# An attention pipeline reordered slot by slot: weighted sum in four places, triangle cleared under two signals, causal mask added from half the array's height

## The chip, the cores and the metric

The kernel is written in Bass and runs on one core of a Trainium2 chip. The metric is the device time of one launch, in microseconds (us). The names of the engines are those of the profile: PE is TensorE (PEld its weight loads), DVE is VectorE, ACT is ScalarE, POOL is GpSimd, and SP is SyncE, which only issues DMA transfers here.

## The reference, cut to what matters

Two transformer-like layers run one after the other; the change touches only the first one's differential attention (8 batches, 512 tokens, 16 heads, two attention maps a head):

```
q1, q2, k1, k2 = heads of x @ Wq1, x @ Wq2, x @ Wk1, x @ Wk2     # 8 features each
v = heads of x @ Wv                                             # 16 features each
a1 = softmax(where(causal, q1 k1^T * scale, -inf))
a2 = softmax(where(causal, q2 k2^T * scale, -inf))
out = (a1 - lam * a2) @ v
merged = layernorm(out) * (1 - LAM_INIT)
return merged @ Wo
```

After it come a feed-forward layer, a state-space scan and a mixture of experts. The change leaves their code as it is.

## The kernel before, in words

The attention works in **rounds**, one for each batch (r = 0 to 7), with a preparing round r = -1 ahead and a draining round r = B behind. A round has 8 **slots** (g = 0 to 7), and each slot works on a **group** of two heads, that is four attention maps. The work is software-pipelined by an order written out by hand. In slot g:

- the *first scores* of group g (`first_pair`, L755): five pairs of 128x512 units, computed only to find each query's largest score. DVE takes the maximum of each unit (L1036), and after ten units the negated maxima (`qneg`, L1047);
- POOL splits the maxima of group g-1 into two bf16 parts (`nsp`, L630 and L632), PE turns them (`turn_neg`, L860), ACT copies them (`nparts`, L704), and SP sends them as two more rows of the query stack (L595);
- the *second scores* of group g-2 (`second_pair`, L807), transposed and with the maximum already subtracted, in five pairs, and ACT's exponential of each unit (L679) into `pT`. POOL clears what lies above the diagonal (L639, three instructions, all counted on the semaphore `masked`);
- the *weighted sum* of group g-3 (`product`, L822): four chunks of keys, c = 0 to 3, with 512, 384, 256 and 128 query columns, summed in the one bank `ob`. It needs `pT` cleared, POOL's copy `vs` of the values (L656), and `ob` read by ACT;
- ACT's copy of the sum of group g-4 out of `ob` (`o_sb`, L685), PE's turn of it (`turn_o`, L852), and ACT's copy of the turned sum (L695).

Beside these a round carries the **preparation** of the next batch: `turn_x` (slot 0), four `project` products of 128x512 (L878, slots 1 to 4), each cut into three bf16 parts by ACT (the high part, L709), DVE (the rest `res`, L1041), ACT (the middle part, L689) and POOL (the lowest part, L660) and stored by SP (L604, six DMAs each), and four `value` products (L884, slots 3 to 6). It also carries the **post-processing** of the batch before: reciprocals (L998), POOL's products and sum (L644 to L648), squares, their sum, a Newton iteration for the inverse root and `merged` (L1010 to L1020) on DVE, then in slot 7 `turn_m0`, `turn_m1` (L892) and the eight products of `wo` (L899), whose result DVE gates and adds to x (L1050, L1054).

The first scores use three PSUM banks (`p1b`), the second scores three others (`p2b`), in turn: a pair of units t may be written when unit 2t-2 has been read. The side products share one bank, `auxb`: each waits until the one before it has been read (`aux_free`). Every engine takes its instructions strictly in the order in which `slot` of its block issues them, so that order sets what waits behind what.

The causal mask of the diagonal units is added by PE ahead of the scores (`mask`, L759): the identity is the stationary operand and `causal`, a 128x512 tile with -3e38 above the diagonal, is the moving one. There are four of these in a slot, for two of the five pairs:

```
def mask(bank):
    pe.matmul(bank[:, :], k.identb[:, :], causal[:, :, :].rearrange("p c t -> p (c t)"), start=True, ...)
```

The order of PE in a slot is given by `AUX`, `AV_AT` and the loop over t: second pair ahead of first pair, the first pair of the *next* slot at the end of this one.

Of the kernel before, what the change touches and what calls it, by code (L numbers as in the profile page):

```python
# [21 lines left out]
P = 128  # L22
# [204 lines left out]
class AttentionTiles:  # L227
# [3 lines left out]
    def __init__(self, nc, ctx, k):  # L231
# [10 lines left out]
        self.causal = sb("causal", [P, TILES, P], BF16)  # L242
# [25 lines left out]
def setup(nc, d, k, t):  # L268

    with ExitStack() as ctx:  # L270
# [50 lines left out]
        def _(pool):  # L321
# [11 lines left out]
            pool.memset(t.causal[:, :, :], 0.0).then_inc(t.slots_set, 1)  # L333
            pool.memset(t.ks[:, :, :, :], 1.0).then_inc(t.slots_set, 1)
            pool.wait_ge(t.slots_set, 3)
            pool.affine_select(out=t.causal[:, :, :], in_=t.causal[:, :, :], compare_op=ALU.is_ge, fill=NEG, base=0,
                               pattern=[[0, TILES], [-1, P]], channel_multiplier=1).then_inc(t.slots_set, 1)
# [107 lines left out]
AUX = {"turn_o": 1, "turn_neg": 2, "project": 3, "value": 4, "turn_x": 4, "turn_m0": 3, "turn_m1": 4, "wo": 5}  # L445
CHUNKS = ((0, 0, S), (1, P, S), (2, 2 * P, S), (3, 3 * P, S))
# [15 lines left out]
def bank_of(g, u):  # L462
    return (g * UNITS + u) % BANKS
# [39 lines left out]
def attention(nc, d, k, t):  # L503
# [3 lines left out]
    with ExitStack() as ctx:  # L507
# [6 lines left out]
        def sem(name):  # L514
            return ctx.enter_context(nc.semaphore(name))

        wqk, causal, xn, hT, parts, res, vst, qs, ks, vs, pT, bmax = (t.wqk, t.causal, t.xn, t.hT, t.parts, t.res, t.vst, t.qs, t.ks, t.vs, t.pT, t.bmax)
# [12 lines left out]
        first_unit, first_read, second_unit, exp_done, masked, vs_ready, av_done, o_read = (  # L530
            sem(n) for n in ("first_unit", "first_read", "second_unit", "exp_done", "masked", "vs_ready", "av_done", "o_read"))
# [43 lines left out]
        def _(sp):  # L575
# [13 lines left out]
            def slot(r, g, on, prep, post):  # L589
# [7 lines left out]
                if prep and 2 <= g < 6:  # L597
                    b, j = r + 1, g - 2
# [14 lines left out]
        def _(pool):  # L613
            for s, n in CREDITS.items():
                pool.sem_inc(s, n)
            def slot(r, g, on, prep, post):
# [4 lines left out]
                alone = isinstance(r, int) and r == B  # L621
                if on(1):
# [6 lines left out]
                    pool.sem_inc(passed, 1)  # L629
                    pool.tensor_copy(high, lowest).then_inc(nsp_high, 1)  # L630
                    pool.wait_ge(nsp_high, G + 1)
                    pool.tensor_tensor(mid, lowest, high, ALU.subtract).then_inc(nsp_ready, 1)  # L632
                if on(3):
                    r3, g3 = lagged(r, g, 3)
                    a = g3 % 2
                    pool.wait_ge(exp_done, (r3 * GROUPS + g3 + 1) * UNITS + BANK_CREDITS)
                    pool.sem_inc(passed, 1)
                    for block_ap, n in ((pT[:, a, :, 0:P], UNITS), (pT[:, a, 1:8:2, 384:512], 4), (pT[:, a, 8:10, 256:384], 2)):
                        pool.affine_select(out=block_ap, in_=block_ap, compare_op=ALU.is_ge, fill=0.0, base=0,  # L639
                                           pattern=[[0, n], [1, P]], channel_multiplier=-1).then_inc(masked, 1)  # L640
# [5 lines left out]
                if post and g == 5 and not alone:  # L646
                    pool.wait_ge(pool_own, pb * 2 + 2)
                    pool.tensor_tensor(og[:, :, :], og[:, :, :], o2[:, :, :], ALU.add).then_inc(og_ready, 1)  # L648
                if on(2):
                    r2, g2 = lagged(r, g, 2)  # L650
                    G = r2 * GROUPS + g2
                    a = g2 % 2
                    pool.wait_ge(aux_read, aux_use(r2 - 1, 6, "value") + 1)
                    pool.wait_ge(av_done, G + 1)
                    pool.sem_inc(passed, 1)
                    pool.tensor_copy(vs[:, a, :, :, :], vst[:, r2 % 2, :, 2 * g2:2 * g2 + 2, :]).then_inc(vs_ready, 1)  # L656
                if prep and 2 <= g < 6:
                    j, J = g - 2, (r + 1) * 4 + g - 2
# [1782 lines left out]
```

## Time and profile before

| what | us |
|---|---|
| median of 3 runs | 1569.78 |
| lowest, highest run | 1566.35, 1570.98 |
| the profiled execution, its own time | 1568.49 |
| its span in the trace | 1566.7 |
| PE busy over the span | 1265.0 (81%) |
| DVE busy | 1162.6 (74%) |
| ACT busy | 1080.8 (69%) |
| POOL busy | 799.6 (51%) |
| first score of the attention starts at | 59.9 |
| first scores end at | about 747 |

The span counts from the first to the last instruction of the core. "Busy" is the union of an engine's instructions; matmuls that run side by side in different parts of the array are counted once there. The mean granted clock of PE is 0.92 of full speed. A timeline row gives start, duration, engine, line, operation, output and inputs, the count of merged instructions, and in brackets how long the engine had been idle before it and who released it.

### The profile page before, as it was taken

The numbers are of one execution on the slowest core, as the hardware profiler recorded it, in microseconds if no ns is written. First come the engines' busy times: TensorE is split into PE (matmuls) and PEld (weight loads), VectorE is DVE, ScalarE is ACT, GpSimd is POOL, SyncE is SP. The second block draws the span as 40 slices with busy tenths as digits, with TensorE's granted clock in tenths as the row PEclk, the third lists the DMA queues.
The fourth block names the chain that finished last, engine by engine and source line by source line (L and its number), as shares of the span: only waits on it lengthen the run. The fifth ranks groups of instructions, "written<-read, shape, count | busy, mean of one in ns | idle before, by whom it ended". The sixth has DMA issues, their size and how long they took to land. (4 is left out here: it accounts for less than half of the span.)

```text
span 1566.7 us, 25959 instructions
## 1 busy us (share of the span) xinstructions
PE 1265.0 (81%) x8518; PEld 567.3 (36%) x8581; DVE 1162.6 (74%) x2000; ACT 1080.8 (69%) x1712; POOL 799.6 (51%) x721
## 2 busy tenths in 40 slices
PE   4588878788888888787777857778668999999998
PEld 3133333333333333333335522323223444444443
DVE  5667676767677676778859689999995677766663
ACT  2167767767675767676667788888537877787776
POOL 3033433525252442534200158988955777787777
PEclk8579999999998999999879979889988999999999
DMA  5332322213132222311000178978748777777785
GB/s 135 92 92 63 89 66 69 86 50 105 42 94 61 75 80 64 91 43 32 2 0 1 56 227 281 311 276 272 266 154 191 177 191 178 177 188 183 192 192 128
DMA packets 123688, 198.60 MB, mean 127 GB/s; under 512 B 24604, under 2 KB 60088, under 8 KB 123576
## 3 DMA queue, kind: packets, MB, share of 16 engines
q1 hardware_dynamic: 122136, 195.08, 43.7%
q10 hardware_dynamic: 1440, 2.10, 0.4%
q8 instruction: 62, 1.02, 0.3%
q14 instruction: 50, 0.41, 0.1%
HBM read 167.76 MB, written 28.84 MB: 125 GB/s over the span
## 5 line engine op out<-in xcount | busy, mean ns | idle before, releaser
L1036 DVE TENSOR_REDUCE bmax<-p1b 128x4 f32<-128x512 f32 x640 | 410.6, 686 | 125.9 <-PE p1b L755 123.2
L679 ACT ACTIVATE pT<-p2b 128x512 f32<-128x512 f32 x640 | 349.2, 603 | 184.2 <-PE p2b L807 183.0
L2179 POOL TENSOR_TENSOR hid_l<-e_hid,w_experts 128x1024 f16<-128x1024 f32 (+1 forms) x136 | 281.3, 2084 | 105.1 <-ACT w_experts L2314 104.2
L2413 DVE TENSOR_TENSOR e_hid<-ub,w_experts 128x1024 f32<-128x1024 f32 x128 | 155.8, 1223 | 122.5 <-ACT ub L2325 113.1
L630 POOL CAST nsp<-qneg 128x16 bf16<-128x16 f32 x64 | 12.7, 198 | 425.0 <-DVE qneg L1047 425.0
L822 PE MATMUL ob<-pT,vs 128*32 128x512 f32 (+3 forms) x2048 | 192.1, 462 | 1.9 <-POOL pT L639 1.2
L1882 PE MATMUL yb<-ch,ident 128*128 128x512 f32 x256 | 138.4, 674 | 49.7 <-POOL ch L1852 49.3
L807 PE MATMUL p2b<-w_high 50*128 50x512 bf16 (+3 forms) x1024 | 130.4, 314 | 48.0 <-ACT pT L679 48.0
L2314 ACT ACTIVATE w_experts<-e_hid 128x1024 f16<-128x1024 f32 (+1 forms) x136 | 139.4, 1026 | 39.1 <-DVE e_hid L2413 39.0
L2325 ACT ACTIVATE ub<-ub 128x1024 f32<-128x1024 f32 (+1 forms) x136 | 133.9, 985 | 37.6 <-PE ub L2230 35.8
L639 POOL TENSOR_SCALAR_AFFINE_SELECT pT<-pT 128x1280 f32<-128x1280 f32 (+2 forms) x192 | 145.3, 790 | 11.7 <-ACT pT L679 11.6
L755 PE MATMUL p1b<-w_high 48*128 48x128 bf16 (+2 forms) x1792 | 133.1, 253 | 19.9 <-DVE bmax L1036 19.8
L2228 PE MATMUL ub<-w,w_high 128*128 (+1 forms) x264 | 100.9, 382 | 22.9 <-DVE e_hid L2413 13.7
L1962 ACT ACTIVATE dA<-dt,nA 128x511 f32<-128x511 f32 x128 | 85.4, 712 | 45.5 <-DVE hs L2025 33.6
L759 PE MATMUL p1b<-causal,identb 128*128 128x512 bf16 x193 | 81.1, 422 | 37.2 <-DVE bmax L1036 25.1
L807 PEld LDWEIGHTS p2b<-w_high 50*128 50x128 bf16 x1024 | 34.7, 95 | 196.7 <-ACT pT L679 149.9
L1852 POOL TENSOR_TENSOR ch<-hs,crow 128x1024 f32<-128x1024 f32 x40 | 93.9, 2352 | 17.2 <-DVE hs L2025 16.8
L2229 PE MATMUL ub<-w,w_high 128*128 (+1 forms) x264 | 100.8, 382 | 0.0
L2230 PE MATMUL ub<-w,w_low 128*128 (+1 forms) x264 | 100.6, 381 | 0.0
L2228 PE MATMUL e_yb<-w_experts,w_high 128*128 128x512 f16 x264 | 100.1, 379 | 0.5 <-POOL hid_l L2179 0.5
L2230 PE MATMUL e_yb<-w_experts,w_low 128*128 128x512 f16 x264 | 100.1, 379 | 0.0
L2229 PE MATMUL e_yb<-hid_l,w_high 128*128 128x512 f16 x264 | 100.1, 379 | 0.0
(308 smaller groups left out, 2265.0 us busy)
## 6 DMA issues: line engine op xcount, KB each, us to landing
w_experts<-shares SPq DMA_DIRECT2D x256, 256.0 KB, 4.3
brow<-bc_rows SPq DMA_DIRECT2D x64, 512.0 KB, 4.0
crow<-bc_rows SPq DMA_DIRECT2D x64, 512.0 KB, 5.2
q_stacks<-w_low SPq DMA_DIRECT2D x96, 128.0 KB
k_stacks<-w_low SPq DMA_DIRECT2D x96, 128.0 KB
w_high<-q_stacks SPq DMA_DIRECT2D x128, 96.0 KB, 2.3
w_high<-k_stacks SPq DMA_DIRECT2D x128, 96.0 KB, 2.3
w_high<-nparts SPq DMA_DIRECT2D x128, 4.0 KB
```

Of the source, the lines that this page charges most:

```text
L639: pool.affine_select(out=block_ap, in_=block_ap, compare_op=ALU.is_ge, fill=0.0, base=0, pattern=[[0, n], [1, P]], channel_multiplier=-1). ...
L679: act.activation(pT[:, g2 % 2, stored(w), :], p2b[bank_of(g2, w)][:, :], ACT.Exp, scale=SCALE).then_inc(exp_done, 1)
L807: mm = pe.matmul(p2b[bank_of(g, 2 * t + j)][:, at:at + S - c * P], ks[rows, slot, head, c * P:(c + 1) * P], qs[rows, slot, head, c * P:S], ...
L822: mm = pe.matmul(ob[32 * m:32 * m + 32, q0:q1], vs[:, a, c, m // 2, :], pT[:, a, u, at:at + q1 - q0], start=(n == 0), stop=(n == len(CHUNK ...
L1036: dve.tensor_reduce(to, bank, AX, ALU.max).then_inc(first_read, 1)
L1882: mm = pe.matmul(yb[:, :], k.ident[:, :], ch[:, m % 4, j, :], start=False, stop=(m == PAIRS - 1 and j == 1), skip_group_check=True)
L2179: pool.tensor_tensor(flat(hid_l[:, rounded(p), 0:n, :]), flat(hid[:, place(p), 0:n, :]), rounded_half(p, 0, n), ALU.subtract).then_inc(spl ...
L2228: pe.matmul(to, w[0], high, start=start, stop=False, skip_group_check=True)
L2229: pe.matmul(to, w[0], low, start=False, stop=False, skip_group_check=True)
L2230: return pe.matmul(to, w[1], high, start=False, stop=stop, skip_group_check=True)
L2314: act.activation(rounded_half(p, 0, n), flat(hid[:, place(p), 0:n, :]), ACT.Copy).then_inc(hid_rounded, 1)
L2413: dve.tensor_tensor(h, u, flat(share[:, p % SHARES, :, :]), ALU.mult).then_inc(hid_ready, 1)
```

## The change

1. **PE's order.** The first pair of a slot is issued in the slot itself, and each pair t is first scores, then second scores. The weighted sum's chunks go to four places: chunk 1 after pair 1, chunks 3 and 2 after pair 2, chunk 0 (512 columns) last. `project` and `turn_m0` move behind pair 0, `turn_x` and `turn_m1` behind pair 1, `turn_o` from behind pair 1 to behind pair 3, `wo` behind pair 4 and ahead of chunk 0.
2. **ACT's order** goes by single units: `o_sb` and the high part right after the first exponential, the middle part and `nparts` after the fifth, the copy of the turned sum after the seventh, the values after the tenth. The middle part is made in the project's own slot, not one later.
3. **POOL's order.** `vs` first, then the sum of `og` (slot 5), then `nsp`, then the clearing of the last two units of group g-3 under a signal of its own (`masked_last`), the products of slot 4, the lowest part, and at the end the clearing of units 0 to 7 of group g-2, one slot earlier than before. Only chunk 2 waits for `masked_last`.
4. **DVE's order.** The rest `res` behind unit 3 instead of 6, the normalisation of x behind unit 0 of slot 0, and the steps of the post-processing at other units.
5. **SP** stores the parts one slot earlier.
6. **The mask.** `later`, a 128x384 tile, is now the stationary operand (64 rows of it) and the identity, 64 rows broadcast to 256 columns, the moving one: four products of 64 rows by 256 columns for a pair, instead of two of 128 rows by 512.

```diff
-        self.causal = sb("causal", [P, TILES, P], BF16)
+        self.later = sb("later", [P, 3, P], BF16)
...
-            def mask(bank):
-                pe.matmul(bank[:, :], k.identb[:, :], causal[:, :, :].rearrange("p c t -> p (c t)"), start=True, stop=False, skip_group_check=True)
+            def mask(bank, j, half):
+                rows = slice(HALF * j, HALF * j + HALF)
+                keys = bank[:, :].rearrange("p (c t) -> p c t", c=TILES)[:, :, HALF * half:HALF * half + HALF]
+                pe.matmul(keys, later[rows, 1 + half - j, :], k.identb[rows, rows].unsqueeze(1).broadcast_to([HALF, TILES, HALF]),
+                          start=(half == 0), stop=False, skip_group_check=True)
...
                 bank_free(r, g, 2 * t + 1)
                 if kind == DIAGONAL:
-                    mask(bank[1])
+                    for half in range(2):
+                        for j in range(2):
+                            mask(bank[j], j, half)
...
-AV_AT = (2, 3, 4, 4)
-O_COPY_AT, OT_AT, NEG_COPY_AT, HIGH_AT, MID_AT, HT_AT, V_COPY_AT, MT_AT = 0, 1, 2, 3, 1, 4, 4, (3, 4)
-RES_AT = 6
-POST_AT = ((4, 0), (5, 6), (5, 8), (6, 0), (6, 2), (6, 4), (6, 6), (6, 8))
+CHUNK_FIRST, CHUNK_LAST = 1, 0
+O_COPY_AT, HIGH_AT, MT_AT, HT_AT, MID_AT, NEG_COPY_AT, OT_AT, V_COPY_AT = 0, 0, (1, 3), 2, 4, 4, 6, 9
+RES_AT, NORM_AT = 3, 0
+POST_AT = ((3, 9), (5, 4), (5, 8), (6, 4), (6, 5), (6, 6), (6, 7), (6, 9))
...
+                if c == CHUNK_FIRST:
+                    pe.wait_ge(masked, 2 * G + 2)
                     pe.wait_ge(vs_ready, G + GROUPS + 2)
                     pe.wait_ge(o_read, G + 1)
+                if c == 2:
+                    pe.wait_ge(masked_last, G + 1)
```

In the rows below, `p1b` is a bank of first scores, `p2b` one of second scores, `ob` the weighted sum and `auxb` the side products.

**PE, the start of slot 6 of a full round.** Before (the slot's first pair was already issued behind the chunks of slot 5, and is shown as the first two rows):

```order
L759 MATMUL p1b<-causal,identb 128x512 x2
L755 MATMUL p1b<-w_high 128x128 x8
L807 MATMUL p2b<-w_high 128x512 x2
L807 MATMUL p2b<-w_high 128x384 x2
L807 MATMUL p2b<-w_high 128x128 x2
L755 MATMUL p1b<-w_high 128x384 x2
L755 MATMUL p1b<-w_high 128x128 x2
L852 MATMUL auxb<-ident,o_sb 128x128 x4
L759 MATMUL p1b<-causal,identb 128x512
L807 MATMUL p2b<-w_high 128x512 x2
L759 MATMUL p1b<-causal,identb 128x512
L755 MATMUL p1b<-w_high 128x128 x8
```

And now:

```order
L767 MATMUL p1b<-identb,later 128x4x64 x4
L760 MATMUL p1b<-w_high 128x128 x8
L813 MATMUL p2b<-w_high 128x512 x2
L760 MATMUL p1b<-w_high 128x384 x2
L760 MATMUL p1b<-w_high 128x128 x2
L813 MATMUL p2b<-w_high 128x384 x2
L813 MATMUL p2b<-w_high 128x128 x2
L831 MATMUL ob<-pT,vs 32x384 x4
L767 MATMUL p1b<-identb,later 128x4x64 x4
L760 MATMUL p1b<-w_high 128x128 x8
L813 MATMUL p2b<-w_high 128x512 x2
```

The turn of `o_sb` between pairs 1 and 2 gave way to chunk 1 of the weighted sum, the masks of a pair stand together, and first and second scores have changed places.

**POOL, from the products of slot 4 to the clearing of slot 5.** Before:

```order
L660 TENSOR_TENSOR w_low<-w_low 128x512 [waits mid_ready]
L630 CAST nsp<-qneg 128x8x2 [waits qneg_ready,aux_done]
L632 TENSOR_TENSOR nsp<-qneg,nsp 128x8x2 [waits nsp_high]
L639 AFFINE_SELECT pT<-pT 128x10x128 [waits exp_done]
L639 AFFINE_SELECT pT<-pT 128x4x128
L639 AFFINE_SELECT pT<-pT 128x2x128
L648 TENSOR_TENSOR og<-og,o 128x1024 [waits pool_own]
L656 COPY vs<-w_experts 128x256 [waits aux_read,av_done]
```

And now:

```order
L660 TENSOR_TENSOR w_low<-w_low 128x512 [waits mid_ready]
L645 AFFINE_SELECT pT<-pT 128x8x128 [waits exp_done]
L645 AFFINE_SELECT pT<-pT 128x4x128
L628 COPY vs<-w_experts 128x256 [waits av_done,aux_read]
L631 TENSOR_TENSOR og<-og,o 128x1024 [waits pool_own]
L639 CAST nsp<-qneg 128x8x2 [waits aux_done,qneg_ready]
L641 TENSOR_TENSOR nsp<-qneg,nsp 128x8x2 [waits nsp_high]
L645 AFFINE_SELECT pT<-pT 128x4x128 [waits exp_done]
```

`vs` and the sum into `og` now stand ahead of the split of the maxima, and eight of the ten units are cleared before the slot ends.

## Rows read from the trace of the kernel before

**Rows 1.** Windows, a slot without preparation: length, busy PE, PEld, DVE, ACT, POOL, then PEclk

```profile
699.61:708.19 8.58, 7.22 (x93) 3.10 (x90) 6.70 (x12) 6.65 (x13) 2.99 (x6) 1.00 0.17 46
```

**Rows 2.** Windows, one full round: slots 1 to 6, 7, then 0; the round; the last round

```profile
329.90:340.62 10.72, 8.92 (x100) 3.71 (x100) 7.29 (x12) 7.39 (x15) 2.99 (x6) 1.00 0.17 47
340.62:350.69 10.07, 8.35 (x95) 3.45 (x90) 7.20 (x12) 7.58 (x15) 4.15 (x7) 1.00 0.18 55
350.69:360.77 10.08, 8.61 (x87) 3.39 (x82) 7.20 (x13) 7.89 (x16) 4.15 (x7) 1.00 0.38 118
360.77:371.96 11.19, 9.05 (x92) 3.63 (x92) 7.90 (x13) 7.97 (x16) 7.99 (x9) 1.00 0.32 96
371.96:382.75 10.79, 8.54 (x100) 3.65 (x100) 9.02 (x14) 7.37 (x15) 7.40 (x8) 1.00 0.37 115
382.75:394.04 11.29, 9.63 (x95) 3.81 (x90) 10.73 (x25) 7.20 (x14) 2.99 (x6) 0.85 0.39 120
394.04:403.05 9.01, 7.76 (x90) 3.62 (x86) 6.61 (x11) 7.63 (x15) 2.99 (x6) 1.00 0.07 17
403.05:418.46 15.41, 12.82 (x107) 6.25 (x109) 9.01 (x17) 7.41 (x14) 2.99 (x6) 0.78 0.10 28
318.21:406.61 88.40, 73.52 (x740) 31.42 (x748) 64.96 (x116) 60.75 (x120) 35.64 (x55) 0.94 0.25 74
...
674.46:750.67 76.21, 62.59 (x711) 27.44 (x718) 61.81 (x107) 54.56 (x107) 29.43 (x50) 0.98 0.12 33
```

**Rows 3.** Timeline, the slot of rows 1: PE and ACT up to the turn of o_sb

```profile
699.67 0.38 PE L807 MATMUL p2b<-w_high 50*128 50x512 bf16 x2
...
700.15 1.09 ACT L679 ACTIVATE pT<-p2b 128x512 f32<-128x512 f32 x2 [1.07 <-PE p2b L807]
...
701.12 0.69 ACT L685 ACTIVATE o_sb<-ob,factor 128x512 f32<-128x512 f32 x1
...
701.86 0.42 PEld L852 LDWEIGHTS auxb<-ident,o_sb 128*128 128x128 f32 x4 [0.73 <-ACT o_sb L685]
```

**Rows 4.** Timeline, the same slot: the rest of PE's queue, and four reductions in a row

```profile
702.99 0.39 PE L759 MATMUL p1b<-causal,identb 128*128 128x512 bf16 x1
...
703.31 0.40 PE L755 MATMUL p1b<-w_high 48*128 48x128 bf16 x8
...
703.86 1.02 PE L822 MATMUL ob<-pT,vs 128*32 128x512 f32 x5
...
704.82 0.39 PE L807 MATMUL p2b<-w_high 50*128 50x384 bf16 x4
...
705.04 0.38 PE L755 MATMUL p1b<-w_high 48*128 48x384 bf16 x4
...
705.46 2.62 DVE L1036 TENSOR_REDUCE bmax<-p1b 128x4 f32<-128x512 f32 x4 [0.43 <-PE p1b L755]
706.14 0.11 PEld L807 LDWEIGHTS p2b<-w_high 50*128 50x128 bf16 x4 [0.62 <-ACT pT L679]
```

**Rows 5.** Timeline, a slot with preparation: the project product and the rest

```profile
336.24 1.13 PE L878 MATMUL auxb<-w_low,wqk 128*128 128x512 f32 x2
...
338.03 0.69 DVE L1041 TENSOR_TENSOR w_low<-auxb,w_low 128x512 f32<-128x512 f32 x1 [1.00 <-ACT w_low L709]
```

**Rows 6.** Timeline, the start of a slot 0, after the products of wo

```profile
408.99 0.61 PE L755 MATMUL p1b<-w_high 48*128 48x384 bf16 x4 [1.68 <-DVE bmax L1036]
```

**Rows 7.** Timeline, the slot of rows 1: the rows of the maxima on their way

```profile
704.06 0.59 ACT L704 ACTIVATE nparts<-auxb 8x512 bf16<-8x512 bf16 x1
704.67 1.27 SPq L595 DMA_DIRECT2D w_high<-nparts  x2
```

**Rows 8.** Windows: where their bytes move; then a slot of round 0, and one two slots later

```profile
706.50:707.00 0.50, 0.50 (x14) 0.23 (x12) 0.47 (x2) 0.43 (x1) 0.00 (x0) 1.00 0.03 8
...
91.00:102.40 11.40, 10.41 (x79) 3.59 (x78) 6.92 (x11) 7.35 (x14) 4.11 (x7) 0.70 0.37 112
113.00:122.00 9.00, 7.65 (x89) 3.38 (x90) 6.74 (x12) 7.27 (x15) 4.15 (x7) 1.00 0.34 103
```

More of the change, by code:

```diff
@@ L621, in slot @@
                 alone = isinstance(r, int) and r == B
+                if on(2):
+                    r2, g2 = lagged(r, g, 2)
+                    G = r2 * GROUPS + g2
+                    a = g2 % 2
+                    pool.wait_ge(aux_read, aux_use(r2 - 1, 6, "value") + 1)
+                    pool.wait_ge(av_done, G + 1)
+                    pool.tensor_copy(vs[:, a, :, :, :], vst[:, r2 % 2, :, 2 * g2:2 * g2 + 2, :]).then_inc(vs_ready, 1)
+                if post and g == 5 and not alone:
+                    pool.wait_ge(pool_own, pb * 2 + 2)
+                    pool.tensor_tensor(og[:, :, :], og[:, :, :], o2[:, :, :], ALU.add).then_inc(og_ready, 1)
                 if on(1):
@@ L645, in slot @@
                     pool.tensor_tensor(o2[:, :, :], o[:, :, 1, :], rcv[:, :, 1].unsqueeze(2).broadcast_to(full), ALU.mult).then_inc(pool_own, 1)
[L646 to L648 removed]
+                if prep and 1 <= g < 5:
+                    j, J = g - 1, (r + 1) * 4 + g - 1
+                    pool.wait_ge(mid_ready, J + 1)
+                    pool.tensor_tensor(parts[:, j % 2, 2, :], res, parts[:, j % 2, 1, :], ALU.subtract).then_inc(split_ready, 1)
                 if on(2):
                     r2, g2 = lagged(r, g, 2)
[L651 removed]
                     a = g2 % 2
[L653 to L658, printed above, removed]
[L659 to L660 removed]
+                    pool.wait_ge(exp_done, (r2 * GROUPS + g2) * UNITS + 8 + BANK_CREDITS)
+                    clear_future(pT[:, a, 0:8, 0:P], [[0, 8]], masked)
+                    clear_future(pT[:, a, 1:8:2, 384:512], [[0, 4]], masked)
             rounds(pool, slot)
@@ L714, in slot @@
                         act.activation(mT[:, c, :], auxb[:, :], ACT.Copy).then_inc(aux_read, 1)
[L715 removed]
+                    if u == V_COPY_AT and prep and 3 <= g < 7:
                         c = g - 3
@@ new lines, in weigh @@
+                def weigh(c):
+                    if on(3):
+                        product(*lagged(r, g, 3), c)
+                pairs(0)
+                if 1 <= g < 5:
+                    side("project")
+                if g == GROUPS - 1:
+                    side("turn_m0")
+                pairs(1)
+                weigh(1)
+                if g == 0:
+                    side("turn_x")
+                if g == GROUPS - 1:
+                    side("turn_m1")
+                pairs(2)
@@ L943, in _ @@
+                side("turn_neg")
+                weigh(3)
+                weigh(2)
+                pairs(3)
+                side("turn_o")
+                pairs(4)
+                if 3 <= g < 7:
+                    side("value")
+                if g == GROUPS - 1:
+                    side("wo")
+                weigh(0)
             rounds(pe, slot)
@@ L951, in slot @@
                 G = r * GROUPS + g
-                if prep and g == 0 and (not isinstance(r, int) or r >= 0):
-                    dve.wait_ge(aux_done, aux_use(r - 1, 0, "turn_x") + 1)
-                    for c in range(TILES):
-                        ins = normalize(dve, k, xn[:, c, :], b * TILES + c)
-                    ins.then_inc(xn_ready, 1)
                 if isinstance(r, int) and r < 0:
@@ L1036, in slot @@
                         dve.tensor_reduce(to, bank, AX, ALU.max).then_inc(first_read, 1)
+                    if prep and (g, u) == (0, NORM_AT) and r >= 0:
+                        dve.wait_ge(aux_done, aux_use(r - 1, 0, "turn_x") + 1)
+                        for c in range(TILES):
+                            ins = normalize(dve, k, xn[:, c, :], b * TILES + c)
+                        ins.then_inc(xn_ready, 1)
                     if prep and u == RES_AT and 1 <= g < 5:
```

129 lines of the change are left out of this document (52 added, 77 removed).

## The prediction

> **What bounds the kernel now.** I read the windows by slot first, then the timeline of one slot, then the windows of the odd slots. The change lies in the attention, which is some 690 of the 1566.7 us; what follows it is left as it is.
>
> In a slot with nothing beside the pipeline [rows 1] TensorE is busy 7.22 of 8.58 us, VectorE 6.70 and ScalarE 6.65. No engine is full, TensorE is nearest. A full round takes 88.40 us, with TensorE busy 73.52, VectorE 64.96 and ScalarE 60.75 [rows 2]. So the bound is TensorE's queue and the waits in it. The timeline shows the one real gap of the plain slot: the second scores start at 699.67, the first exponential 0.48 later, ScalarE does two of them before it copies `o_sb` (0.97), and the turn of it starts 0.74 after that copy began [rows 3]. That is 2.19 us in which TensorE has one pair of each kind to do. From there its queue is dense [rows 4]. The other losses of a round are in slots 5 and 6, where VectorE is busy 9.02 and 10.73 us, and in slots 7 and 0 (9.01 + 15.41 us), where VectorE waits for `wo`, then normalises, while the granted clock is 0.78 [rows 2]; there TensorE stands 1.68 us for a bank [rows 6].
>
> **The change, part by part.**
>
> *Masks.* A full-height mask costs 0.32 us from its start to that of the scores behind it (702.99 to 703.31), four in a slot: about 1.2 us. The same 512 columns of half-height scores cost 0.22 (704.82 to 705.04) [rows 4]. That two half-height products with different rows run side by side is seen in the scores: eight of 128 columns take 0.40 us including the last one's latency. A pair's four products of 256 columns should therefore stream in 2 x 0.107 = 0.21 us, and I charge 0.3 with the first weight load. The bounds: 0.2 (nothing but streaming) and 0.6 (two full masks as now, no gain). I take 0.3, since it is next to the 0.22 row. Two pairs: 0.6 in place of 1.2, so TensorE's own work in a plain slot falls from 7.2 to 6.6 us.
>
> *Plain slot.* I walk TensorE's queue from the masks of pair 0. Masks 0.3, scores 0.24: second scores at 0.55. First exponential at 1.03 (+0.48), `o_sb` at 1.57, since now only one exponential (half of 1.09) stands ahead of it; the sum's chunk 1, which needs `ob` free, can start at 2.3 (+0.74) [rows 3]. Pair 1 fits in between: its first scores wait for the maximum of unit 0 (0.3 + 0.43 + 0.65 = 1.4, a reduction taking a quarter of 2.62 [rows 4]), its second ones for the exponential until 1.7. From 2.3: chunk 1 0.78, masks and pair 2 0.3 + 0.33 + 0.25, `turn_neg` 0.12, chunks 3 and 2 0.78, pair 3 0.47, `turn_o` 0.5, pair 4 0.57 with 0.1 of waiting for a maximum, chunk 0 1.06. The next slot begins at 7.6, and I take 7.7: 0.9 less than 8.58, of which 0.6 are masks and 0.3 the copy behind one exponential. The neighbours: VectorE needs ten reductions of 0.65 and 0.24 for `qneg`, 6.8; ScalarE about 6.9. Both fit in 7.7 but have under 1 us left, so no larger gain can come from TensorE.
>
> *Project, slots 1 to 4.* The product is 1.13 us long [rows 5]. Behind pair 0 it fills the wait for the first maximum (0.8 to 1.4), so 0.4 to 0.5 of it shows. The high part delays ScalarE by 0.6, and with it the exponentials of pair 1; the rest (0.69) sits behind unit 3 and holds `turn_neg` until 4.3. Walked through, the next slot starts at 8.4. With a value product (0.62 between pair 4 and chunk 0, slots 3 and 4): 9.1. Now these four slots take 42.1 us [rows 2]; then 35.0.
>
> *Slots 5 and 6* are VectorE's: 6.8 of its own, 2.5 of squares and sum in slot 5, 3.9 in slot 6. I expect 9.4 and 10.2 in place of 10.79 and 11.29 [rows 2], for its waits at the slot ends shrink but its work stays. The moved queues: GpSimd's sum into `og` (2.4 us) stands ahead of `nsp` in slot 5, and slot 4 ends late there (its products, lowest part and clearing come to 8 to 9 us). `nsp` is then ready some 3.5 us into the slot, `turn_neg` is due at 4: covered, but it costs what it is late. SyncE's six stores (3.7 us of issuing) come one slot earlier behind `split_ready`, and the next rows of maxima 4 us after: covered.
>
> *Slots 7 and 0.* `wo` runs behind pair 4, while VectorE still has two maxima and `qneg` to do, and chunk 0 runs while VectorE gates and adds; before, both stood in the way of the next slot. Walk: slot 7 11.3, slot 0 8.7, so 20.0 in place of 24.4 [rows 2]. The idle stretch of rows 6 should go.
>
> *The sum.* Round: 35.0 + 9.4 + 10.2 + 20.0 = 74.6. The same walk done on the slot of 10.07 gives 9.6, 4% too short, so I add 3%: 77. Six such rounds: 6 x (88.4 - 77) = 68. The last round, without preparation [rows 2]: 76.2 to 71, 5. Round 0: its first slots run at a clock of 0.5 to 0.7 and take 11.4 [rows 8], where masks cost twice; 1.5 each for five slots, 1 each for three: 10. The preparing round has the middle part ahead of the values: 1.5. The drain: 1. Together 85.5 us off 1568.5, the profiled execution's own time: 1483. The median of the runs shown lies 1.3 above that execution, which changes nothing.
>
> **A rule on the masks.** The full-height mask's 0.32 against 0.22 for the same columns at half height [rows 4] is a step of 0.1 where the height of the tile changes. The Trainium skill, TensorEngine Tiling (Array Packing), Key Properties, says that changing the tiling mode drains the engine. By that rule, the trace agrees.
>
> **The rivals.**
>
> *A. Masks cheaper still.* The drains between masks and scores vanish altogether, so a mask pair costs 0.2: 0.1 less, twice in 62 slots with TensorE as the bound, 12 us more: 1471. For it the 0.22 row; against it that pair 0 and pair 2 follow the sum, whose tiles are of another shape, so one change stays at each. 0.12.
>
> *B. Masks no cheaper.* The four half products run one behind the other, as their banks and weight loads alternate; 0.25 more for each pair, 0.5 a slot, 54 slots: 27 us, 1510. Against it: the scores of rows 4 alternate in the same way, side by side. This is also the case in which that part of the change does not do what it says. 0.08.
>
> *C. The rows of maxima come late.* `nparts` starts at 704.06, and the last of its bytes move in the window 706.5 to 707.0, 2.8 us later, with 4.2 to the second scores that need them [rows 7, 8]. In the new slot it is 3.6 (4.7 to 8.3), so 0.8 is left. If ScalarE comes to `nparts` later than walked, TensorE stands still at the start of the next slot. At 0.7 us in each slot that is 43 us: 1526. Its cousins, a late clearing or a late `vs`, would cost alike. 0.12.
>
> *D. The clock, slower than before.* TensorE fell to its lower level (1.2 GHz of 2.4) after idle stretches [rows 2, 6], and a slot at mean 0.70 took 11.4 against 9.0 at 1.00 [rows 8]. The change takes a third of the streamed mask work away and puts small waits (0.6 at pair 0, 0.4 at chunk 1) into each slot. At the lower level a slot's 6.6 us of work grows by some 5. Then it decides from 17 slots on (85/5); in half of the 64 slots it costs 160 and gives 1643, and if only the slots 5 to 0 of each round are hit, 28 of them, 140: about 1623. Against it: plain slots before have a gap of 0.9 us and keep 1.00 [rows 1], the new gaps are shorter, and the longest one goes. The Trainium skill, TensorE: Matmul & The Clock Gate, Part 1, says that the throttled state is the default and that recent activity lifts it; by it, less work in a slot speaks for this case. 0.04.
>
> *E. No change.* All engines coupled anew, each gain met by a wait of the same size: 1569. 0.02.
>
> **How the numbers follow.** The forecast has 0.62, and its time is 1483. Its own bounds: with half of the 3% allowance for waits that I do not see, 1475; with three times it, 1500. To hold 8 in 10, the range takes in A, B and C's milder half: 1458 to 1525 (the lower end is a round of 73.5 with A). Faster by over 0.3% (the least that a measurement of this kernel can tell from no change): the forecast, A, B, C, 0.94. Within it, 0.02. Slower, D, 0.04.
>
> **What would show it.** Right: a plain slot of 7.6 to 7.9 us in the last round; half-height mask products whose four starts lie within 0.25 us and whose group is busy about 35 us less; full rounds of 75 to 79 us; slots 7 and 0 together near 20 with a clock above 0.9; no wait on the rows of maxima. Wrong: TensorE idle ahead of its second scores at a slot's start (C), ahead of chunk 1 for more than 0.5 us, a clock under 0.9 over a full round (D), masks that take 0.5 us a pair (B), or slots 1 to 4 above 9.5, which would mean that ScalarE's high and middle parts sit on the path.

## The result, and the profile after

| | before | after |
|---|---|---|
| median of the runs | 1568.93 | 1449.97 |
| lowest, highest | 1566.35, 1570.98 | 1447.97, 1452.15 |
| the profiled execution, its own time | 1568.49 | 1447.97 |
| mean granted clock of PE | 0.920 | 0.939 |

The changed kernel is 119 us faster: ratio 0.9249, interval 0.9232 to 0.9265. The forecast was a gain of 85.5 us and 1483; the result lies 8 us below the range. The direction came out as forecast, and so did the mechanism of the plain slot; the size did not. Groups of instructions of the profile's page (busy us, mean ns of one | idle time ahead, releaser), two lines of before, then after:

```profile
L1036 DVE TENSOR_REDUCE bmax<-p1b 128x4 f32<-128x512 f32 x640 | 410.6, 686 | 125.9 <-PE p1b L755 123.2
L679 ACT ACTIVATE pT<-p2b 128x512 f32<-128x512 f32 x640 | 349.2, 603 | 184.2 <-PE p2b L807 183.0
```

```profile
PE 1200.6 (83%) x8837; PEld 562.0 (39%) x8837; DVE 1156.0 (80%) x2000; ACT 1072.2 (74%) x1712; POOL 801.6 (55%) x721
...
L1055 DVE TENSOR_REDUCE bmax<-p1b 128x4 f32<-128x512 f32 x640 | 406.9, 685 | 64.0 <-PE p1b L760 58.2
L684 ACT ACTIVATE pT<-p2b 128x512 f32<-128x512 f32 x640 | 349.3, 599 | 97.5 <-PE p2b L813 97.3
```

VectorE and ScalarE do nearly the work they did (within 9 us), in 120 us less. What went is their waiting: VectorE stood idle ahead of the maxima for 125.9 us before and 64.0 now, ScalarE ahead of the exponentials for 184.2 and 97.5. TensorE's recorded work fell by 64 us, 29.3 of them in the masks. The lines view of PE, before and after:

```profile
L759 PE MATMUL p1b<-causal,identb 128*128 128x512 bf16 x193 | 81.1, 422 | 37.2 <-DVE bmax L1036 25.1 <-PEq L841 8.6 <-issue 2.5
```

```profile
L767 PE MATMUL p1b<-identb,later 64*128 64x256 bf16 x512 | 51.8, 281 | 19.3 <-DVE bmax L1055 12.6 <-DMA w_high<-k_stacks 6.6
```

The trace before holds 193 of the 256 full masks (the records of the others are missing), so 29.3 is a lower bound.

Windows after, slots counted from one `qneg` to the next as in [rows 1, 2]: a plain slot of the last round (8.58 before), then slots 1 to 7 and the slot 0 behind them, a full round, and the last round (columns as in [rows 1]):

```profile
573.72:581.20 7.48, 6.68 (x98) 3.11 (x96) 6.50 (x11) 6.59 (x14) 2.96 (x7) 1.00 0.20 54
...
428.18:436.14 7.96, 7.69 (x100) 3.38 (x98) 7.10 (x12) 7.41 (x16) 4.12 (x8) 1.00 0.16 49
436.14:444.20 8.06, 7.77 (x100) 3.48 (x98) 7.11 (x13) 7.45 (x16) 4.14 (x8) 1.00 0.52 150
444.20:452.97 8.77, 8.50 (x108) 3.85 (x104) 7.91 (x13) 7.78 (x17) 4.93 (x10) 1.00 0.49 148
452.97:460.76 7.79, 7.52 (x90) 3.22 (x84) 7.03 (x13) 7.34 (x16) 7.18 (x9) 1.00 0.44 143
460.76:471.10 10.34, 8.53 (x112) 3.89 (x108) 8.95 (x14) 7.38 (x16) 7.38 (x10) 1.00 0.49 147
471.10:482.67 11.57, 8.35 (x103) 3.89 (x98) 11.02 (x25) 7.77 (x16) 3.08 (x6) 1.00 0.15 43
482.67:491.76 9.09, 8.20 (x86) 4.67 (x86) 6.49 (x12) 6.94 (x14) 1.84 (x4) 0.81 0.02 5
491.76:502.11 10.35, 9.32 (x119) 4.54 (x119) 9.21 (x18) 7.18 (x15) 3.17 (x7) 1.00 0.15 44
419.33:493.27 73.94, 65.86 (x784) 30.91 (x780) 64.82 (x115) 59.26 (x119) 35.83 (x55) 0.98 0.29 88
565.76:636.64 70.88, 59.95 (x764) 28.85 (x760) 61.08 (x107) 54.27 (x106) 31.23 (x51) 0.95 0.13 37
```

In the plain slot all three engines are close to full: 6.68, 6.50 and 6.59 of 7.48 us. In slots 5 and 6 VectorE has 8.95 and 11.02 us: it is the bound there, as before.

Where the 120.5 us between the two profiled executions lie, by the start of the addition to x that ends each batch's post-processing (231.0 and 674.5 us before, 199.7 and 565.8 after, for the first and the sixth):

| stretch | forecast | measured |
|---|---|---|
| to the first such addition (preparing round, round 0, most of the first full round) | 23 | 31.3 |
| five full rounds | 57 | 77.4 |
| last round | 5 | 5.3 |
| drain | 1 | -0.2 |
| everything behind the attention | 0 | 6.7 |

The last line lies in code that is the same in both kernels. It took between 767.7 and 775.8 us over the profiles of all kernels here, 774.6 before and 767.9 after, and nearly all of the difference lies in the state-space scan (from its first to its last instruction 247.4 and 242.0 us). Whether that is spread or a consequence of the change is open: `changed_again`, which by its expectation was to come above 770 if it was spread, came at 768.1.

### The profile page after: what moved, and what is told of

Same layout as the page of the kernel before. It is cut to its first block and busy times, and to the rows that moved or that the text cites. A ratio compares the mean times of both kernels' runs of the same rounds, so it can differ in the third digit from the quotient of the medians.

```text
span 1446.2 us, 26470 instructions
## 1 busy us (share of the span) xinstructions
PE 1200.6 (83%) x8837; PEld 562.0 (39%) x8837; DVE 1156.0 (80%) x2000; ACT 1072.2 (74%) x1712; POOL 801.6 (55%) x721
## 5 line engine op out<-in xcount | busy, mean ns | idle before, releaser
L684 ACT ACTIVATE pT<-p2b 128x512 f32<-128x512 f32 x640 | 349.3, 599 | 97.5 <-PE p2b L813 97.3
L645 POOL TENSOR_SCALAR_AFFINE_SELECT pT<-pT 128x512 f32<-128x512 f32 (+1 forms) x192 | 148.0, 787 | 201.9 <-ACT pT L684 201.9
L831 PE MATMUL ob<-pT,vs 128*32 128x384 f32 (+3 forms) x2048 | 185.7, 447 | 8.3 <-ACT o_sb L690 6.5
L1906 PE MATMUL yb<-ch,ident 128*128 128x512 f32 x256 | 134.5, 655 | 45.8 <-POOL ch L1876 45.5
L760 PE MATMUL p1b<-w_high 48*128 48x128 bf16 (+2 forms) x1792 | 129.0, 246 | 37.3 <-DVE bmax L1055 37.1
L813 PE MATMUL p2b<-w_high 50*128 50x512 bf16 (+3 forms) x1024 | 124.8, 301 | 2.4 <-ACT pT L684 1.9
L1986 ACT ACTIVATE dA<-dt,nA 128x511 f32<-128x511 f32 x128 | 85.5, 712 | 46.7 <-DVE hs L2049 34.7
L760 PEld LDWEIGHTS p1b<-w_high 48*128 48x128 bf16 x1792 | 63.4, 96 | 115.6 <-DVE bmax L1055 97.7
L1906 PEld LDWEIGHTS yb<-ch,ident 128*128 128x128 f32 x256 | 47.2, 200 | 121.7 <-POOL ch L1876 76.3
L2049 DVE TENSOR_TENSOR_SCAN hs<-dA,dBx 128x1024 f32<-128x1024 f32 x40 | 91.4, 2284 | 3.4 <-ACT dA L1986 0.6
```

Source lines behind the costliest of these rows:

```text
L684: act.activation(pT[:, g2 % 2, stored(u), :], p2b[bank_of(g2, u)][:, :], ACT.Exp, scale=SCALE).then_inc(exp_done, 1)
L760: return pe.matmul(bank[:, at * P:(at + blocks[1] - blocks[0]) * P], qs[rows, slot, head, c * P:(c + 1) * P], ks[rows, slot, head, blocks[ ...
L831: mm = pe.matmul(ob[32 * m:32 * m + 32, q0:q1], vs[:, a, c, m // 2, :], pT[:, a, u, at:at + q1 - q0], start=(c == CHUNK_FIRST), stop=(c == ...
L1906: mm = pe.matmul(yb[:, :], k.ident[:, :], ch[:, m % 4, j, :], start=False, stop=(m == PAIRS - 1 and j == 1), skip_group_check=True)
```

## The experiments

### How much the masks are, and how much the order

The same change with the full-height masks (`new_full_masks`); the old order with half-height masks (`old_half_masks`); since these have to stand together ahead of a pair's scores, where the old order put each mask behind its own bank, the old order with full masks put together (`old_full_masks_together`) as its control; and the new order without masks (`new_no_masks`).

```diff
-                    for half in range(2):
-                        for j in range(2):
-                            mask(bank[j], j, half)
+                    for j in range(2):
+                        mask(bank[j])
```

> The changed kernel with the old full-height masks (identity stationary, 512 columns moving), four a slot, all in front of their pair. Theory 1, the order carries most of the 119 us and the masks a quarter: a half-height mask pair took 0.23 us in the changed trace, two full ones took 0.54 in the old one, so 0.6 us a slot come back in the some 52 slots that TensorE bounds: about 1450 + 31 = 1481 (1470 to 1492). Theory 2, the masks carry half or more, since the forecast fell short by 34 us and the mask term (0.3 a pair) was the one that was set too high: 1505 or more. Theory 3, the new order leaves TensorE so much slack that masks are hidden: 1455 or less.

> The kernel before with the half-height masks, all four of a pair in front of it (the old order issues one full mask of pair 2 ahead of the second scores; here both come behind them). Theory 1: 0.6 us a slot off TensorE's queue in the slots it bounds (8.58 to about 8.0 us in the plain slot), 30 us in all: 1539 (1528 to 1550). Theory 2: 1510 or less. Theory 3 (the old order waits elsewhere, the masks are covered): 1560 or more.

> A control for the run before: the kernel before with its full masks, only moved together in front of their pair. Theory 1: the mask that used to run ahead of the second scores of pair 2 filled 0.3 us of waiting, so 0 to 0.3 us a slot are lost: 1569 to 1588. If it comes below 1560, the placing itself was a gain and must be taken off the run before.

> The changed kernel without any mask product on the first scores, so the maxima also take in later keys (the masks are left out of the computation; the products, reductions and everything after stay). Theory 1: what is left of the masks is 2 x 0.23 us a slot on TensorE's queue, and VectorE, busy 6.5 to 6.9 of 7.5 in a plain slot, takes over as the bound: 10 to 25 us, 1425 to 1440. Theory 2 (masks still weigh): 1415 or less. Theory 3: 1447 to 1452, no change.

Measured, beside a before of 1567.02:

| kernel | median us | ratio, interval |
|---|---|---|
| new_full_masks | 1483.87 | 0.9449, 0.9417 to 0.9482 |
| old_half_masks | 1552.59 | 0.9905, 0.9877 to 0.9932 |
| old_full_masks_together | 1591.37 | 1.0160, 1.0129 to 1.0190 |
| new_no_masks | 1440.41 | 0.9179, 0.9149 to 0.9209 |

So the order alone gives 83 us, and the half-height masks 34 on top of it (31 by the ratios). My forecast had 0.6 us a slot for them, which over the 54 slots of rival B is 32: that term was right. `old_half_masks` came out slower than expected (1552.6, where 1528 to 1550 was expected), and so did its control (1591.4, for 1569 to 1588). In the old order the half-height masks give 39 against this control, but the control costs 24 against before; that a mask ahead of both banks has to wait for the later one may be the reason, and was not tried by itself. In its profile a plain slot grew by only 0.14 us (8.58 to 8.72), and in one full round slots 2, 3 and 5, which kept the clock before, are longer at a lower one (0.74 to 0.86). Only 9.5 us are left in the masks, just under the 10 to 25 expected. A pair with full masks (timeline of new_full_masks), then one with half-height masks (of the changed kernel):

```profile
589.25 0.59 PE L764 MATMUL p1b<-causal,identb 128*128 128x512 bf16 x2
589.77 0.40 PE L760 MATMUL p1b<-w_high 48*128 48x128 bf16 x8
```

```profile
573.41 0.39 PE L767 MATMUL p1b<-identb,later 64*128 64x256 bf16 x4
573.64 0.39 PE L760 MATMUL p1b<-w_high 48*128 48x128 bf16 x8
```

0.52 us from mask to scores against 0.23, where I had 0.3. Four half-height products of 256 columns, two side by side, stream in 0.21, so almost nothing is left between them and the scores, which use 48 rows; behind the full-height masks there is some 0.1 more than their 2 x 0.21 (these figures are estimates, columns over 2.4 GHz). By the rule of the Trainium skill, TensorEngine Tiling (Array Packing), Key Properties, a change of tiling mode drains the array, and another tile of the same mode does not; the trace agrees on both sides.

### Which part of the order carries it

Four kernels, each the changed one with one piece put back: `sum_copied_later` (copy of the sum and high part behind the second exponential, not the first), `triangle_cleared_later` (all of a group cleared a slot later, behind the split; chunk 1 waits for the first two of the three instructions), `weighted_sum_at_the_end` (the four chunks together behind pair 4), `wo_behind_the_sum` (chunk 0 ahead of `wo`).

```diff
-O_COPY_AT, HIGH_AT, MT_AT, HT_AT, MID_AT, NEG_COPY_AT, OT_AT, V_COPY_AT = 0, 0, (1, 3), 2, 4, 4, 6, 9
+O_COPY_AT, HIGH_AT, MT_AT, HT_AT, MID_AT, NEG_COPY_AT, OT_AT, V_COPY_AT = 1, 1, (1, 3), 2, 4, 4, 6, 9
```

```diff
+                    clear_future(pT[:, g3 % 2, 0:8, 0:P], [[0, 8]], masked)
+                    clear_future(pT[:, g3 % 2, 1:8:2, 384:512], [[0, 4]], masked)
...
-                if on(2):
-                    r2, g2 = lagged(r, g, 2)
-                    a = g2 % 2
-                    pool.wait_ge(exp_done, (r2 * GROUPS + g2) * UNITS + 8 + BANK_CREDITS)
-                    clear_future(pT[:, a, 0:8, 0:P], [[0, 8]], masked)
-                    clear_future(pT[:, a, 1:8:2, 384:512], [[0, 4]], masked)
```

```diff
-                weigh(1)
...
-                weigh(3)
-                weigh(2)
...
+                weigh(1)
+                weigh(3)
+                weigh(2)
                 weigh(0)
```

> The changed kernel with ScalarE's copy of the sum (and of the project's high part) behind the second exponential instead of the first. Theory 1 (the forecast's walk: chunk 1 starts 0.74 us after that copy and all of TensorE's queue hangs on it): 0.5 us later in each of some 52 slots, 1450 + 26 = 1476 (1466 to 1484). Theory 2 (VectorE now holds the slot, as 9.5 us for no masks at all suggest, so the queue has slack): at most 0.2 a slot, 1450 to 1460.

> The changed kernel with all of the clearing back in the later slot, behind nsp, in three instructions (1.09 + 0.64 + 0.64 us), chunk 1 waiting for the first two. In the changed trace nsp ends some 2.0 us into a slot and chunk 1 starts at 2.3, so clearing would end at 3.7 to 3.9. Theory 1: chunk 1 and all behind it move by 1.4 us, 0.8 to 1.4 a slot: 1505 to 1540. Theory 2 (slack, as above): 0.5 a slot, 1470 to 1485. Theory 3, the two signals are not needed: 1455 or less.

> The changed kernel with the four chunks of the weighted sum in one place, at the end of the slot, in the same order. Nothing else moves. Theory 1 (the places matter: the chunks fill the waits for maxima, and 2.7 us of them in a row starve VectorE and ScalarE, which get no new unit): 0.8 to 1.5 us a slot, 1500 to 1545. Theory 2 (it is the first-before-second order and the early side products that gain, the places little): 1450 to 1475.

> The changed kernel with the eight products of wo behind chunk 0 in slot 7 instead of ahead of it. Theory 1 (the forecast: chunk 0 covers VectorE's gating and adding): VectorE gates 1.0 us later in 8 rounds and normalises later, 5 to 8 us: 1455 to 1460. Theory 2 (VectorE has the next slot's first units late anyway, or the order within slot 7 does not matter): 1449 to 1453.

Measured, beside a before of 1569.92:

| kernel | median us | over the changed kernel | ratio, interval |
|---|---|---|---|
| sum_copied_later | 1467.45 | 17.5 | 0.9349, 0.9325 to 0.9373 |
| triangle_cleared_later | 1520.93 | 71 | 0.9693, 0.9664 to 0.9722 |
| weighted_sum_at_the_end | 1538.15 | 88 | 0.9793, 0.9771 to 0.9815 |
| wo_behind_the_sum | 1453.37 | 3.4 | 0.9259, 0.9234 to 0.9285 |

The copy behind one exponential is worth 0.3 us a slot on average, the number of my plain slot. It is not even: the two plain slots of the last round take 7.97 and 8.04 us in place of 7.48 and 7.56, so 0.5 each, and the slots with preparation 0.2 to 0.3 more. The next two are far larger than the whole forecast allowed them, and with the masks they add up to more than the change gives: each piece needs the others. With the triangle cleared later, TensorE stands at chunk 1 in every slot. Waits of its queue from 100 to 600 us (us in total, times, longest), and one such chunk:

```profile
PE ob L827 <- POOL pT L645: 50.0, 49, 4.3
...
634.28 0.85 PE L827 MATMUL ob<-pT,vs 128*32 128x384 f32 x8 [0.79 <-POOL pT L645]
```

The same chunk in a slot 5, with GpSimd's queue ahead of it (`og`, the split, the clearing):

```profile
419.64 2.35 POOL L631 TENSOR_TENSOR og<-og,o 128x1024 f32<-128x1024 f32 x1
...
422.21 1.19 POOL L641 TENSOR_TENSOR nsp<-qneg,nsp 128x16 bf16<-128x16 f32 x1
423.36 2.27 POOL L645 TENSOR_SCALAR_AFFINE_SELECT pT<-pT 128x1024 f32<-128x1024 f32 x3
...
425.09 1.51 PE L827 MATMUL ob<-pT,vs 128*32 128x384 f32 x8 [4.02 <-POOL pT L645]
```

The mean of the 49 waits is 1.02 us, but they are unequal: 0.3 to 0.4 us in slots 1 to 4, 0.6 to 1.0 in slots 6, 7 and 0, and 4.0 or more in slot 5 of a full round, where the clearing now stands behind the sum into `og` and the split; slot 5 holds half of the 50 us. That slot takes 15.6 us in most rounds in place of 10.3, part of it at a lower clock (mean 0.78), which is some 35 of the 71 us. So my theory 1, 0.8 to 1.4 us in every slot, met the total by luck: slots 1 to 4 lost 0.3 to 0.5 us each. Chunk 1 this early needs GpSimd to have done eight of ten units in the slot before, above all in slot 5. With the chunks together, TensorE's queue holds both neighbours up. One block, and the first exponential behind it:

```profile
651.82 2.36 PE L831 MATMUL ob<-pT,vs 128*32 128x384 f32 x32
...
655.04 0.60 ACT L684 ACTIVATE pT<-p2b 128x512 f32<-128x512 f32 x1 [1.88 <-PE p2b L813]
```

Waits of this kernel and of the changed one, from 100 to 600 us in both:

```profile
ACT pT L684 <- PE p2b L813: 139.8, 60, 4.7
DVE bmax L1055 <- PE p1b L760: 109.9, 101, 4.5
```

```profile
ACT pT L684 <- PE p2b L813: 80.6, 99, 2.8
...
DVE bmax L1055 <- PE p1b L760: 43.8, 98, 2.3
```

The waits are longer (ScalarE's also fewer, VectorE's as many), 59 and 66 us more in all. In slots 1 and 2 that is 1.2 to 1.3 us a slot at full clock (9.25 in place of 7.97 and 8.05); in the slots 5 and 6 the granted clock fell as well (means of 0.75 to 0.91), which is part of the 88. So the places of the chunks are what keeps both neighbours fed: scores come between the first chunk, the middle two and the last. `wo` ahead of chunk 0 is worth 3.4 us by the medians, but the intervals of the two ratios overlap, and the changed kernel once more came to 1452.15 (next section). For it speaks the trace: slot 0 of the full rounds takes 10.84 us, in place of 10.35 (once 10.59).

### Slots 5 and 6, where the forecast was too good

These two took 21.9 us where I had 19.6, from `qneg` to `qneg`. In slot 5 of the changed kernel:

```profile
461.74 2.49 DVE L1055 TENSOR_REDUCE bmax<-p1b 128x4 f32<-128x512 f32 x4 [0.73 <-PE p1b L760]
461.92 2.36 POOL L631 TENSOR_TENSOR og<-og,o 128x1024 f32<-128x1024 f32 x1
...
464.22 0.20 POOL L639 CAST nsp<-qneg 128x16 bf16<-128x16 f32 x1
464.31 1.22 DVE L1029 TENSOR_TENSOR sq<-og 128x1024 f32<-128x1024 f32 x1
464.50 1.12 POOL L641 TENSOR_TENSOR nsp<-qneg,nsp 128x16 bf16<-128x16 f32 x1
...
465.67 0.33 PE L869 MATMUL auxb<-identb,nsp 128*8 128x128 bf16 x3 [0.71 <-POOL nsp L641]
```

The second instruction of the split takes 1.12 us on 128x16, and TensorE waits 0.71 for it. It does so in seven of its 64 executions, each time behind VectorE's squares; the others take 0.22. A control and four kernels went after it and after VectorE's work: `changed_again`; `squares_on_scalar` (ScalarE squares `og` behind the fourth exponential of slot 5); `squares_scalar_merged_pool` (also `merged` on GpSimd in slot 6); and then, with both of these, `squares_awaited_later` (VectorE awaits the squares at unit 8, not 4) and `maxima_ahead_of_og` (also GpSimd's split ahead of the sum into `og`, and the squares behind the sixth exponential).

```diff
+                    if u == SQ_AT and post and g == 5:
+                        act.wait_ge(og_ready, pb + 3)
+                        act.activation(sq[:, :, :], og[:, :, :], ACT.Square).then_inc(sq_ready, 1)
...
-                        dve.wait_ge(og_ready, pb + 3)
-                        link(dve.tensor_tensor(sq[:, :, :], og[:, :, :], og[:, :, :], ALU.mult))
+                        dve.wait_ge(sq_ready, pb + 1)
+                        dve.sem_inc(dve_post, 1)
```

```diff
+                if post and g == 6 and not alone:
+                    pool.wait_ge(aux_done, aux_use(r - 1, GROUPS - 1, "turn_m1") + 1)
+                    pool.wait_ge(dve_post, (pb + 1) * POST_LINKS)
+                    pool.tensor_tensor(merged[:, :, :].rearrange("p c (h e) -> p (c h) e", e=VD), og[:, :, :],
+                                       orstd[:, :].unsqueeze(2).broadcast_to(full), ALU.mult).then_inc(merged_ready, 1)
```

> The changed kernel once more, beside the next two. All theories: 1448 to 1453. It also tells how far the part behind the attention, which no kernel here changes and which took 767.7 to 775.3 us in ten profiled executions, varies from run to run: if it comes above 770 here, the 6.7 us by which it was shorter in the first profile of the changed kernel are not the change's.

> The changed kernel with the squares of slot 5 (1.22 us on VectorE) made by ScalarE behind its fourth exponential. Theory 1 (slots 5 and 6 are VectorE's: busy 8.95 of 10.34 and 11.02 of 11.57): slot 5 falls by 0.8 to 1.2 us in 8 rounds, 1450 - 8 = 1442 (1439 to 1446). Rival (ScalarE's exponentials, pushed back by 1 us, hold TensorE's second scores instead): 1448 to 1456.

> As the run before, and the last product of the post-processing (1.22 us on VectorE at the end of slot 6) made by GpSimd behind its clearing, its constant factor applied by ScalarE's copy of the turned result. Theory 1: slot 6 falls by about 1.2 us in 7 rounds, and TensorE, which stood 1.55 and 0.69 us in slot 6 before its clock fell for part of slot 7 (mean 0.81), may keep it: 1430 to 1437. Rival (GpSimd needs 2.4 us for it, ends later than VectorE did, and the first turn in slot 7 waits): 1440 to 1448.

> As squares_scalar_merged_pool (1440.5), but VectorE waits for the squares only ahead of their sum, four units later. Theory 1 (slot 5 is VectorE's, and it stood 1.52 us for the squares in the run before): slot 5 falls from 10.04 to about 9, 8 us in all: 1432 (1430 to 1436). Rival (slot 5 is held by the split of the maxima behind GpSimd's sum, and the turn that waits for it): slot 5 stays above 9.7, 1438 to 1441.

> As the run before, with GpSimd's split of the maxima ahead of its sum into og in slot 5, and ScalarE's squares two units later. If VectorE alone held slot 5: as the run before, within 2 us. If the split held it too: slot 5 falls to about 8.6, 3 to 8 us more: 1425 to 1430.

Measured, the first three beside a before of 1568.56, the last two beside 1569.78, with slots 5 and 6 of the same round:

| kernel | median us | ratio, interval | slot 5 | slot 6 |
|---|---|---|---|---|
| changed_again | 1452.15 | 0.9268, 0.9243 to 0.9292 | 10.34 | 11.57 |
| squares_on_scalar | 1449.08 | 0.9247, 0.9223 to 0.9271 | 10.04 | 11.57 |
| squares_scalar_merged_pool | 1440.49 | 0.9191, 0.9164 to 0.9219 | 10.03 | 10.44 |
| squares_awaited_later | 1439.42 | 0.9166, 0.9130 to 0.9202 | 9.45 | 10.43 |
| maxima_ahead_of_og | 1441.89 | 0.9177, 0.9144 to 0.9210 | 9.53 | 10.68 |

None of the four came inside the range of its first theory. Taking 1.2 us of squares away from VectorE alone gave 0.3: it waited for them on ScalarE instead (1.52 us at unit 4). With the wait put later slot 5 fell to 9.45, which is my 9.4, and the same instruction of the split is at 0.22 while the squares run on ScalarE (at most 0.28 in all 64 executions, in `squares_on_scalar` as well):

```profile
460.57 0.22 POOL L642 TENSOR_TENSOR nsp<-qneg,nsp 128x16 bf16<-128x16 f32 x1
460.58 1.09 ACT L723 ACTIVATE sq<-og 128x1024 f32<-128x1024 f32 x1
...
460.96 0.33 PE L878 MATMUL auxb<-identb,nsp 128*8 128x128 bf16 x3
```

Yet the time did not follow, 1439.4 after 1440.5. Slot 5 gave 3.9 us over seven rounds in the profile. But there the first score of the attention started 2.5 us later (58.5 for 56.0), in code that is the same, the slots of round 0 took 0.7 us more, slot 7 took 0.7 us more in all (8.94 in place of 8.10 in some rounds of either kernel), and the code behind the attention 1.8 less. A gain of this size is not told apart from such differences. Putting the split ahead of the sum gave nothing more: the sum's place holds slot 5 no further, or what it gave was taken back by the squares' later place, behind which TensorE waited 0.51 us for the exponentials. These two edits were not tried apart. `merged` on GpSimd gave 1.1 us in slot 6, of which slot 7 took 0.5 back (8.10, where 7.64 was the changed kernel's best). The best of these are 10 to 12 us faster than the changed kernel.

## Why the prediction was right and wrong

**Right.** *Masks:* 34 us against 32, and 0.23 a pair against 0.3. *Plain slot:* 7.48 and 7.56 us against 7.7 (the next two, with the reciprocals at the end of the first, 8.29 and 6.98), with `o_sb` and chunk 1 where the walk put them: 1.43 and 2.25 us after the masks (574.84 and 575.66, behind 573.41), against 1.57 and 2.3. *Slots 7 and 0:* 19.4 us, or 18.0 in rounds whose slot 7 takes 7.6, against 20.0. *Last round:* 5.3 against 5.

**The step that failed is the sum of the full round**, 77 us where five rounds average 73.2 (before: 88.7), and with it the first stretch. It has four parts; for the round of 73.9 shown above they are:

- *The 3% allowance*, 2.4 us, was not needed: the walk without it, 74.6, was itself above what came. I took it from a walk of the old slot that came out 4% short. In slots 1 to 4 of the new order TensorE is busy 7.5 to 8.5 us of each slot's 7.8 to 8.8, which leaves no room for waits that I had not walked.
- *Slots 1 to 4*: 32.6 against 35.0, 2.4. One part is that I charged ScalarE's copies and exponentials with their durations. In slot 1, the high part, then four exponentials:

```profile
429.86 0.60 ACT L703 ACTIVATE w_low<-auxb 128x512 bf16<-128x512 f32 x1
430.34 2.17 ACT L684 ACTIVATE pT<-p2b 128x512 f32<-128x512 f32 x4
...
432.41 0.62 ACT L707 ACTIVATE w_low<-w_low 128x512 bf16<-128x512 f32 x1
432.93 0.57 ACT L714 ACTIVATE nparts<-auxb 8x512 bf16<-8x512 bf16 x1
```

  Each has a duration of 0.6 and the next starts 0.48 to 0.52 behind it. The row that would have told was at hand: two merged exponentials take 1.09 [rows 3], not 1.2. So the high and middle parts delay what follows by a half each, not by 0.6: 0.2 us a slot. The plain slot inside them was 7.5 where I had 7.7, another 0.2. Cut at TensorE's first mask, as the walk was, slots 1 to 4 of this round take 7.97, 8.05, 8.60 and 8.60, where I walked 8.4, 8.4, 9.1 and 9.1; the last 0.1 in slots 3 and 4 is the value product (0.63 in the queue, 0.7 in the walk).
- *Slots 7 and 0*: 19.4 against 20.0, 0.6.
- *Slots 5 and 6*: 21.9 against 19.6, 2.3 the other way. In slot 5 it is the split that VectorE's squares slow and their place among the maxima, shown by 10.34 falling to 9.45 once both were changed. I had the split ready 3.5 us into the slot and called it covered; it was ready 4.5 us behind the slot's first mask (465.62 behind 461.09), and 0.9 of that is the slowing, which I did not have. In slot 6 VectorE is busy 11.02 us where I had 10.7 in all and a slot of 10.2: less than its own busy time, an error that the sum of rows would have caught.

2.4 + 2.4 + 0.6 - 2.3 is 3.1, and 4.5 in the shorter rounds; 3.8 on average, 19 us in five (the table's 20.4 has 1.5 more, since the five rounds before averaged 88.7, not 88.4). How this splits depends on where a slot is cut: by TensorE's first masks the same round gives 33.2 for slots 1 to 4, 19.9 for slots 5 and 6, and 20.9 for slots 7 and 0 (19.4 in rounds that keep the clock). By either cut slots 1 to 4 are 1.8 to 2.4 short of the walk and the allowance stands for nothing; by the second cut the error in slots 5 and 6 is only 0.3.

In the first stretch the first mask starts at 56.1, not 59.3, so the preparing round seems to have given 3.2 us, not 1.5; but over the profiles of all kernels with the new order that start lies anywhere between 55.5 and 59.2 (with the old order between 59.2 and 59.6), so this term is uncertain by as much. The full round in it gave a further 3 to 4, and the slots at the lower clock came to 8.9 to 9.2 us, where 11.4 less my 1.5 is 9.9. That makes the 8 us there. The remaining 7 lies behind the attention, and its cause is open. What each of these few tenths in round 0 comes from was not tried.

**The rivals.** A was half right: the pair costs 0.23, and that is some 0.07 us twice a slot, 8 to 9 us. B fell, by new_full_masks. C fell: no wait on the rows of the maxima appears. A neighbour of it does, small: masks, now the first instruction of a slot, wait for the key stacks, 6.6 us in the whole run (L767 above). D fell, the clock rose. In long rounds it still drops in slot 7, behind two waits of TensorE for a bank in slot 6 that VectorE has yet to read:

```profile
478.06 0.39 PE L760 MATMUL p1b<-w_high 48*128 48x256 bf16 x4 [1.55 <-DVE bmax L1055]
...
480.98 0.39 PE L767 MATMUL p1b<-identb,later 64*128 64x256 bf16 x4 [0.69 <-DVE bmax L1055]
```

Slot 7 then has a mean clock of 0.81 and 9.09 us, and 7.6 in rounds without the drop. But those rounds have the same two waits, as this one, whose slot 7 keeps 1.00:

```profile
405.56 0.39 PE L760 MATMUL p1b<-w_high 48*128 48x256 bf16 x4 [1.55 <-DVE bmax L1055]
...
408.49 0.39 PE L767 MATMUL p1b<-identb,later 64*128 64x256 bf16 x4 [0.69 <-DVE bmax L1055]
```

All six full rounds have them and the clock fell behind three, so the waits alone do not decide it; what does is not shown. E fell.

The range failed too. Its lower end stood on a round of 73.5, and the rounds came out at 73.2: it allowed nothing beyond that for round 0 and the preparing round (15.8 us together, forecast 11.5) nor for the code behind the attention (6.7). An allowance that could only make the time longer had no counterpart. At its upper side a sum was off: three times the allowance is 4.8 us more in six rounds, 1512, not 1500.

## What to carry to other kernels

When a queue is walked, charge an engine the start-to-start distance of merged rows, not the duration of one instruction, and let an allowance for unseen waits go both ways in the range. Pieces of a reordering don't add up: put back alone, single pieces cost 71 and 88 us of a gain of 119, since an early chunk needs an early clearing. Look where such a price falls before naming its cause: half of the 71 lay in one slot of eight, where the moved work met a queue that was already late. Moving work off the busiest engine helps only if the place where that engine waits for it moves too.

## What the runs showed of the hardware

- A GpSimd instruction on 128x16 took 1.12 us instead of 0.22 while VectorE ran a product with two operands in SBUF, in all seven of its executions that met one: it started 0.19 us behind VectorE's (464.50, 464.31) and ended at 465.62, 0.09 behind VectorE's end at 465.53. With the squares on ScalarE it took 0.22 to 0.28. The Trainium skill, SBUF — State Buffer, SBUF: two separate sides, calls the port pair that the two engines share an exclusive lock for the whole instruction, taken also by a VectorE operation with two SBUF inputs against a GpSimd one that reads SBUF; the trace agrees.
- From masks of 128 rows to scores of 48 rows took some 0.1 us more than the masks' streaming, behind one mask (0.32 us) and behind two (0.52); from masks of 64 rows to the same scores next to nothing more (0.23).
- Behind the same two waits of TensorE (1.55 and 0.69 us) its granted clock fell in three of six rounds of one run and stayed at 1.00 in the other three.
- ScalarE started a new 128x512 copy or exponential every 0.48 to 0.52 us (rows of slot 1 above), at a duration of 0.6; VectorE's reductions of that size followed every 0.60 (four end after 2.49), at a mean duration of 0.685.
